# Two transformer layers on one core: every attention score product of the first four sequences is computed twice into the same banks

## The chip, the core and the metric

The kernel runs on one core of a Trainium2 chip. Five engines work side by side, each through its own list of instructions in a fixed order, and they wait for one another by semaphores: TensorE (PE in the profile; its weight loads are shown apart as PEld), VectorE (DVE), ScalarE (ACT), GpSimd (POOL) and SyncE (SP, which here issues transfers). TensorE writes its products to PSUM, eight banks of 512 fp32 values for each of 128 partitions, and DVE and ACT read them from there. The metric is the device time of one execution in microseconds (us), lower is better.

## What is computed

Two layers over x of 8 sequences, 512 positions, 128 features, all fp32 at the interface. Each layer is attention with 16 heads of 8 features and then a mixture of 8 experts; both are modulated by a small conditioning product. Layer 0 is what the change touches:

```python
h = _layernorm(x) * (1 + ca) + sa
qkv = jnp.einsum('bnd,ed->bne', h, w_qkv).reshape(b, n, 3, 16, 8)
q, k, v = (qkv[:, :, i].transpose(0, 2, 1, 3) for i in range(3))
attn = jax.nn.softmax(jnp.einsum('bhid,bhjd->bhij', q, k) * SCALE, axis=-1)
out = jnp.einsum('bhij,bhjd->bhid', attn, v)
x = x + ga * (out.transpose(0, 2, 1, 3).reshape(b, n, 128) @ w_out.T + b_out)
h = _layernorm(x) * (1 + cb) + sb
x = x + gb * ffn(h)      # gate, best 2 of 8 experts, one shared expert
```

Layer 1 has the same form, with a causal mask in the attention.

## The kernel before

**Steps.** Each sequence of each layer is a pass i, 0 to 7 for layer 0 and 8 to 15 for layer 1. A pass goes through normalisation (`p_...`), projection, scores, softmax, the product with the values, output projection (`t_...`), second normalisation and gate (`f_...`), the shared expert (`s_...`) and the routed experts (`x_...`). Passes overlap: while one is at its softmax, the next one's scores are computed, and the experts of earlier passes lie between them.

**Scores, computed two ways.** Queries and keys are split into three bf16 parts each, so that a product over 48 rows (`KA`) gives the score of one head to near fp32. For the softmax the kernel needs the maximum of each query's row first. So there is one score product with queries on the partitions, for the maximum alone (`score`, line 834), and a second one with keys on the partitions and three more rows that subtract the maximum (`bscore`, line 856), whose exponential goes into the product with the values.

- A unit `("score", i, f, pr, t)` is one half f of the heads, one of four pairs of heads pr and one of four tiles of 128 queries t: 32 units to a pass of layer 0. It opens two neighbouring PSUM banks and fills each with one matmul, 48 rows by 128 queries against 512 keys. The two matmuls of a unit (a = 0, 1) use different rows of the array. The last matmul raises the semaphore `score`.
- `rowmax` (line 1082, DVE) waits for that semaphore, reduces both banks (128 partitions by 1024 values) and by that frees them.
- After a half of the heads, `max_turn` (line 846) transposes the maxima; a chain over ACT, DVE, POOL and DMA brings them to the tiles QS.
- `bscore` (line 856) also opens two banks; `expo` (line 1429, ACT) takes the exponential of both into ES and frees them; `pv` (line 873) multiplies four heads of ES by the values, eight records in the trace to a unit.

Other rows that matter: line 748 is any dense projection (`product`), line 905 the gate's product, line 1075 the split of a projection on DVE, line 1354 the normalisation on ACT.

**What sets the order.** `plan()` lists every step with its engine, an estimated weight, an urgency (with tables of nudges) and its predecessors; `Plan.settle()` walks this list greedily and fixes each engine's order, and which banks each step opens. A step that opens banks waits for the steps that emptied them (`open_banks`). The weight of a `score` step in this plan is `0.01 + 0.22 * n / 512`.

The loop that issues a score unit:

```python
for t1, c, n in parts:
    for a in range(2):
        r = 64 * a
        mm = eng.matmul(psum[:, bank[u][a], c:c + n], QS[m][r:r + KA, pr, 128 * t1:128 * t1 + 128],
                        KS[m][r:r + KA, pr, 0:n], start=True, stop=i < NB)
...
mm.then_inc(s["score"], 1)
```

Of the kernel before, what the change touches and what calls it, by code (L numbers as in the profile page):

```python
# [13 lines left out]
NB, S, D = 8, 512, 128  # L14
# [27 lines left out]
KA, KB = 6 * DH, 6 * DH + 3  # L42
# [175 lines left out]


PIPE, WAKE = 1.0, 0.65  # L220
WARM = 12, 3, 3
LATER, SPARE = 0.6, 0.05
WEARLY = 0.2
# [313 lines left out]
def program(nc, xin, cT, wm, w0, we, ws, w1, wr1, wr2, wy, bo, out):  # L537
    ctx = ExitStack()
    with ctx:
# [22 lines left out]
        codeq = sb("codeq", [128, 128], BF16)  # L562
        codek = sb("codek", [128, 128], BF16)
# [3 lines left out]
        QS = [sb(f"QS{i}", [128, 4, S], BF16) for i in range(NSTK)]  # L567
        KS = [sb(f"KS{i}", [128, 4, S], BF16) for i in range(NSTK)]
# [60 lines left out]
        psum = ctx.enter_context(nc.psum_tensor("ps", [128, 8, 512], F32))  # L629
# [30 lines left out]
        todo, bank, emptied, _, strips = plan()  # L660
# [19 lines left out]
        for k in UNITS:  # L680
            m = (UNIT[k] if LAYER[k[0]] == 0 else k[1]) % (NST if LAYER[k[0]] == 0 else 2)
# [60 lines left out]
        def _(eng):  # L742
# [22 lines left out]
            for u in todo["PE"]:  # L765
# [4 lines left out]
                elif k in ("p_turn", "f_turn"):  # L770
                    w, i = (0, u[1]) if k == "p_turn" else (1, u[1])
# [3 lines left out]
                    for t in range(NT):  # L775
                        mm = eng.transpose(ps(*u)[:, 128 * t:128 * t + 128], xn[w][:, t, :], ident[:, :])  # L776
                    mm.then_inc(s[k], 1)
                elif k == "m_mm":
# [4 lines left out]
                    for c in range(6):  # L783
                        if l == 0:
                            warm(1)
                        mm = eng.matmul(ps(*u)[:, 8 * c:8 * c + 8], wms[l][c // 3][:, 128 * (c % 3):128 * (c % 3) + 128],
                                        cs[:, l, 0, :], start=True, stop=True)
                    mm.then_inc(s["m_mm"], 1)
                elif k == "m_gm":
# [4 lines left out]
                    for n, c in enumerate((2, 3, 4, 5)):  # L794
                        mm = eng.matmul(ps(*u)[0:8, 128 * n:128 * n + 128], cs[:, l, 0, :],
                                        wms[l][c // 3][:, 128 * (c % 3):128 * (c % 3) + 128], start=True, stop=True)
                    mm.then_inc(s["m_gm"], 1)
                elif k == "w_mm":
# [4 lines left out]
                               start=True, stop=True).then_inc(s[k], 1)  # L803
                elif k == "p_proj":
                    i, n = u[1:]
# [6 lines left out]
                elif k == "p_v":  # L812
                    i = u[1]
# [4 lines left out]
                    for t in range(NT):  # L818
                        mm = product(u, ps(*u)[:, 128 * t:128 * t + 128], hP[:, 128 * t:128 * t + 128],
                                        ws[:, W["v"]:W["v"] + 128], start=True, stop=True)  # L820
                    mm.then_inc(s[k], 1)
                elif k == "score":
                    i, f, pr, t = u[1:]
                    m = (2 * i + f) % NSTK

                    parts = [(t, 0, S)] if i < NB else [(t, 0, 128 * (t + 1))] if t > 1 else [(0, 0, 128), (1, 128, 256)]
                    q.wait_ge(*(on("early", i) if (i, f) == (0, 0) and pr < 2 else on("stack", i, f)))
                    open_banks(u)
                    if i >= NB:
                        q.wait_ge(s["ld", "c_code"], 32)  # L830
                    for t1, c, n in parts:
                        for a in range(2):
                            r = 64 * a
                            mm = eng.matmul(psum[:, bank[u][a], c:c + n], QS[m][r:r + KA, pr, 128 * t1:128 * t1 + 128],  # L834
                                            KS[m][r:r + KA, pr, 0:n], start=True, stop=i < NB)
                        if i >= NB:
                            for a in range(2):
                                r = 64 * a
                                mm = eng.matmul(psum[:, bank[u][a], c + n - 128:c + n], codeq[r:r + 64, :], codek[r:r + 64, :],  # L839
                                                start=False, stop=True)  # L840
                    mm.then_inc(s["score"], 1)
                elif k == "max_turn":
                    i, f = u[1:]
# [3 lines left out]
                elif k == "bscore":  # L847
                    i, f, g, j, pp = u[1:]
                    pr, m = 2 * g + pp, (2 * i + f) % NSTK
                    q.wait_ge(*on("max_ld", i, f))  # L850
                    q.wait_ge(s["ld", "c_ks"], 32 * NSTK)
                    open_banks(u)
                    for j1, c, q0 in key_tiles(i, j):
                        for a in range(2):
                            r = 64 * a
                            mm = eng.matmul(psum[:, bank[u][a], c:c + S - q0], KS[m][r:r + KB, pr, 128 * j1:128 * j1 + 128],  # L856
                                            QS[m][r:r + KB, pr, q0:S], start=True, stop=i < NB)
                        if i >= NB:
                            for a in range(2):
                                r = 64 * a  # L860
                                mm = eng.matmul(psum[:, bank[u][a], c:c + 128], codek[r:r + 64, :], codeq[r:r + 64, :],  # L861
                                                start=False, stop=True)
                    mm.then_inc(s["bscore"], 1)
                elif k == "pv":
                    i, g, j = u[1:]
# [4 lines left out]
                    for j1, c, q0 in key_tiles(i, j):  # L870
                        for a in range(4):
                            q.wait_ge(*on("expo", i, g // 2, g % 2, j, a // 2))
                            mm = eng.matmul(psum[32 * a:32 * a + 9, b, q0:S], VS[i % 3][:, j1, 4 * g + a, :],  # L873
                                            ES[(2 * EXP[i, g, j] + a // 2) % NES][:, a % 2, c:c + S - q0],
                                            start=(j1 == 0), stop=(j1 == NT - 1), skip_group_check=True)
                    mm.then_inc(s["pv"], 1)
                elif k == "v_turn":
# [3 lines left out]
                    for t in range(NT):  # L881
                        mm = eng.transpose(ps(*u)[:, 128 * t:128 * t + 128], US[g % 2][:, 128 * t:128 * t + 128], ident[:, :])
# [1047 lines left out]
```

## Time and profile before

| | us |
|---|---|
| median of 3 timed runs | 1061.68 (1061.51 to 1062.42) |
| the profiled execution, its own time | 1055.22 |
| its span in the trace | 1053.5 |
| PE busy | 976.7 (93%), 10743 matmuls |
| DVE busy | 824.4 (78%) |
| ACT busy | 743.0 (71%) |
| POOL busy | 454.5 (43%) |
| mean granted clock of TensorE | 0.967 |

The profile gives, for each engine, the busy time; TensorE's granted clock as a share of full speed (1.00 is 2.4 GHz, 0.50 is 1.2 GHz); and the chain of work that ended last, followed back from the end. How to read the views used below:

- The table by stretches has, for each stretch, its length, then the busy time and the count of instructions in brackets for PE, PEld, DVE, ACT and POOL, then the granted clock, the share of the DMA engines and GB/s.
- In the timeline a row gives start, length, engine, line, operation, tiles written and read, and in square brackets how long the engine was idle before it and who ended that. Neighbours of one line are merged: x2 is one score unit, x4 two, x8 one `pv` unit.
- In the chain a row gives start, length, engine, tile, line, count.

### The profile page before, as it was taken

The page shows a single profiled execution, that of the slowest core. Times are in us where ns is not written, and L with a number is a line of the kernel's source. Part 1 is how long each engine was busy: PE and PEld are TensorE (multiplying, and loading weights), DVE is VectorE, ACT ScalarE, POOL GpSimd, SP SyncE. Part 2 cuts the span into 40 slices and gives each one's busy share as a digit, 9 for nine tenths or more (in the row PEclk, how much of TensorE's full clock was granted, in tenths as well). Part 3 has the DMA queues.
Part 4 walks back from the last instruction along what each step waited for, and adds up shares of the span by engine and source line. Part 5 has one row for each costly group of instructions (what it writes and reads, how often), then busy time and mean ns, then how long its engine had stood idle before and what let it go on. Part 6 is the DMA issues. An engine that isn't in the chain of part 4 may idle for free.

```text
span 1053.5 us, 27436 instructions
## 1 busy us (share of the span) xinstructions
PE 976.7 (93%) x10743; PEld 529.7 (50%) x10743; DVE 824.4 (78%) x1672; ACT 743.0 (71%) x1225; POOL 454.5 (43%) x545
## 2 busy tenths in 40 slices
PE   7678898879999999999999999999999999999997
PEld 5211222222645455345655666666765555455565
DVE  6888899787999888678977688777877567677456
ACT  4347876668575766987577775666866988877864
POOL 5130121144024435641344742456644566836553
PEclk9858998899999999999999999999999989999999
DMA  6832525254664686584765896777887857411000
GB/s 186 209 115 53 144 73 147 77 168 128 186 204 121 216 247 178 157 246 147 244 203 165 259 278 196 223 208 227 262 260 227 234 167 183 111 62 56 33 12 21
DMA packets 120480, 174.73 MB, mean 166 GB/s; under 512 B 19896, under 2 KB 84280, under 8 KB 120352
## 3 DMA queue, kind: packets, MB, share of 16 engines
q1 hardware_dynamic: 114096, 159.87, 51.3%
q0 software_dynamic: 5680, 12.33, 4.0%
q8 instruction: 85, 1.39, 0.6%
q10 hardware_dynamic: 576, 0.79, 0.3%
q14 instruction: 43, 0.35, 0.1%
HBM read 114.21 MB, written 58.59 MB: 164 GB/s over the span
## 4 chain that ended last, share of the span: by engine, by line
PE 58%; DVE 20%; DMA 7%; ACT 6%; issue 5%; POOL 3%; SPq 1%; POOLq 0%; DVEq 0%; ACTq 0%
PE ps L748 19%; PE ps L873 13%; DVE nm L1082 12%; PE ps L750 8%; PE ps L856 7%; PE ps L834 6%; ACT ES L1429 3%; DMA gr<-d_y,pos 2%; DMA d_h<-hx,pos 1%; ACT xn L1354 1%; DMA d_h<-r,pos 1%; PE ps L776 1%; PE ps L905 1%; PE ps L839 1%; DMA DR<-d_r 1%
## 5 line engine op out<-in xcount | busy, mean ns | idle before, releaser
L1082 DVE TENSOR_REDUCE nm<-ps 128x2 f32<-128x1024 f32 (+3 forms) x512 | 504.6, 1019 | 106.9 <-PE ps L839 63.0
L1429 ACT ACTIVATE ES<-ps 128x1024 f32<-128x1024 f32 (+1 forms) x448 | 418.1, 961 | 104.4 <-PE ps L856 67.2
L873 PE MATMUL ps<-ES,VS 128*9 128x512 f32 (+3 forms) x2048 | 223.2, 522 | 0.4 <-DVE r L1268 0.2
L834 PE MATMUL ps<-KS,QS 48*128 48x512 bf16 (+3 forms) x1024 | 173.4, 354 | 31.0 <-DVE nm L1082 19.5
L856 PE MATMUL ps<-QS,KS 51*128 51x512 bf16 (+3 forms) x1024 | 168.6, 348 | 12.7 <-DVE nm L1082 6.4
L834 PEld LDWEIGHTS ps<-KS,QS 48*128 48x128 bf16 x1024 | 49.1, 94 | 145.9 <-DVE nm L1082 51.1
L856 PEld LDWEIGHTS ps<-QS,KS 51*128 51x128 bf16 x1024 | 50.2, 94 | 137.1 <-ACT ES L1429 44.7
L748 PE MATMUL ps<-hsT,wst 128*128 128x128 f32 x784 | 111.1, 285 | 2.8 <-DVE r L1275 1.6
L1657 POOL DMA_INDIRECT gr<-d_y,pos x80 | 83.3, 1041 | 64.2 <-DMA gr<-d_y,pos 35.7
L748 PEld LDWEIGHTS ps<-hsT,wst 128*128 128x128 f32 x784 | 95.2, 191 | 21.2 <-issue 17.4
L1583 POOL TENSOR_TENSOR sp<-sr,sp 128x512 bf16<-128x512 f32 x32 | 37.2, 1171 | 85.2 <-ACT sp L1390 85.1
L873 PEld LDWEIGHTS ps<-ES,VS 128*9 128x9 f32 x2048 | 37.9, 89 | 66.8 <-issue 57.1
L1468 ACT ACTIVATE tx<-ps 128x384 f32<-128x384 f32 x92 | 44.9, 488 | 34.4 <-PE ps L748 20.8
L1633 POOL DMA_INDIRECT d_h<-hx,pos x40 | 40.4, 1010 | 65.5 <-DMA d_h<-hx,pos 33.4
L1680 POOL TENSOR_TENSOR ya<-ya,yS 128x512 f32<-128x512 f32 x35 | 45.0, 1285 | 46.0 <-DVE yS L1317 45.9
L1633 POOL DMA_INDIRECT d_h<-r,pos x40 | 39.4, 985 | 44.7 <-DMA d_h<-r,pos 27.5
L1354 ACT ACTIVATE xn<-X,rs 128x128 f32<-128x128 f32 x128 | 52.5, 485 | 8.6 <-POOL rs L1579 7.2
L1587 POOL TENSOR_TENSOR nmp<-nmr,nmp 32x128 bf16<-32x128 f32 x32 | 14.0, 437 | 96.7 <-ACT nmp L1408 96.3
L839 PE MATMUL ps<-codek,codeq 64*128 64x128 bf16 x512 | 52.6, 218 | 0.0
L750 PE MATMUL ps<-hsT,wst 128*32 128x128 f32 x1464 | 49.2, 274 | 1.3 <-issue 1.2
L750 PEld LDWEIGHTS ps<-hsT,wst 128*32 128x32 f32 x1464 | 40.0, 110 | 19.7 <-issue 16.8
L861 PE MATMUL ps<-codeq,codek 64*128 64x128 bf16 x512 | 49.7, 218 | 0.1
(229 smaller groups left out, 1541.8 us busy)
## 6 DMA issues: line engine op xcount, KB each, us to landing
wst<-we SPq DMA_DIRECT2D x92, 576.0 KB
d_u<-US SPq DMA_DIRECT2D x60, 256.0 KB
KS<-d_k SPq DMA_DIRECT2D x62, 192.0 KB, 4.8
QS<-d_q SPq DMA_DIRECT2D x62, 192.0 KB, 5.4
hs<-d_h SPq DMA_DIRECT2D x25, 256.0 KB
d_y<-ys SPq DMA_DIRECT2D x25, 256.0 KB, 5.6
d_q<-sp SPq DMA_DIRECT2D x16, 384.0 KB, 3.0
d_k<-sp SPq DMA_DIRECT2D x16, 384.0 KB, 3.7
```

The source lines that it names most:

```text
L748: return eng.matmul(to, lhsT, rhs, start=start, stop=stop)
L750: mm = eng.matmul(to[r:r + 32, :], lhsT[:, r:r + 32], rhs, start=start, stop=stop, skip_group_check=True)
L834: mm = eng.matmul(psum[:, bank[u][a], c:c + n], QS[m][r:r + KA, pr, 128 * t1:128 * t1 + 128], KS[m][r:r + KA, pr, 0:n], start=True, stop=i ...
L839: mm = eng.matmul(psum[:, bank[u][a], c + n - 128:c + n], codeq[r:r + 64, :], codek[r:r + 64, :], start=False, stop=True)
L856: mm = eng.matmul(psum[:, bank[u][a], c:c + S - q0], KS[m][r:r + KB, pr, 128 * j1:128 * j1 + 128], QS[m][r:r + KB, pr, q0:S], start=True, ...
L861: mm = eng.matmul(psum[:, bank[u][a], c:c + 128], codek[r:r + 64, :], codeq[r:r + 64, :], start=False, stop=True)
L873: mm = eng.matmul(psum[32 * a:32 * a + 9, b, q0:S], VS[i % 3][:, j1, 4 * g + a, :], ES[(2 * EXP[i, g, j] + a // 2) % NES][:, a % 2, c:c + ...
L1082: ins = eng.tensor_reduce(nm[f][:, :].rearrange("p (a c) -> p a c", a=2)[:, :, 4 * pr + t1], ps2("score", i, f, pr, t)[:, :, c:c + n], AX. ...
L1354: ins = eng.activation(xn[w][:, t, :], X[:, NT * b + t, :], ACT.Identity, bias=rs[:, m, 2, t:t + 1], scale=rs[:, m, 1, t:t + 1])
L1429: eng.activation(ES[(2 * n + pp) % NES][:, :, 0:w], ps2("bscore", i, f, g, j, pp)[:, :, 0:w], ACT.Exp, scale=SC1 if i >= NB else SC0).then ...
L1633: eng.indirect_dma_start(out=d_h[:, :], out_offset=bass.IndirectOffsetOnAxis(ap=pos[p % 2][:, c, t8:t8 + 1], axis=0), in_=hx[t8 // NT][:, ...
L1657: eng.indirect_dma_start(out=gr[m][:, :], out_offset=None, in_=d_y[p][:, :], in_offset=bass.IndirectOffsetOnAxis(ap=pos[p % 2][:, c, t8:t8 ...
```

## The change

For the passes i = 0 to 3 the loop that issues a score unit runs twice. A table `MORE_S` holds a 1 for each of the 128 units of these passes (i, f, pr, t); a second table, `MORE_B`, of the same kind for `bscore`, is empty. Both matmuls of a unit are issued a second time, with the same operands into the same two banks and with start=True, so that the second result overwrites the first with the same values. The semaphore is raised by the last matmul of the second round. The planner's weights, its order and the banks are as before.

```diff
 PIPE, WAKE = 1.0, 0.65
+MORE_S = {
+    (0, 0, 0, 0): 1, (0, 0, 0, 1): 1, (0, 0, 0, 2): 1, (0, 0, 0, 3): 1, (0, 0, 1, 0): 1, (0, 0, 1, 1): 1,
...
+    (3, 1, 3, 2): 1, (3, 1, 3, 3): 1,
+}
+MORE_B = {
+
+}
...
                     open_banks(u)
                     if i >= NB:
                         q.wait_ge(s["ld", "c_code"], 32)
-                    for t1, c, n in parts:
-                        for a in range(2):
-                            r = 64 * a
-                            mm = eng.matmul(psum[:, bank[u][a], c:c + n], QS[m][r:r + KA, pr, 128 * t1:128 * t1 + 128],
-                                            KS[m][r:r + KA, pr, 0:n], start=True, stop=i < NB)
...
+                    for _ in range(1 + MORE_S.get(u[1:], 0)):
+                        for t1, c, n in parts:
                             for a in range(2):
                                 r = 64 * a
...
+                                mm = eng.matmul(psum[:, bank[u][a], c:c + n], QS[m][r:r + KA, pr, 128 * t1:128 * t1 + 128],
+                                                KS[m][r:r + KA, pr, 0:n], start=True, stop=i < NB)
...
                     mm.then_inc(s["score"], 1)
```

Nothing else in the program moves. On TensorE, where the softmax of pass 0 meets the scores of pass 1, there stood in a row (L834 `score`, L856 `bscore`, L873 `pv`; in the program's own order a `pv` unit has four matmuls):

```order
L856 MATMUL ps<-QS,KS 128x512 x2
L834 MATMUL ps<-KS,QS 128x512 x2
L873 MATMUL ps<-ES,VS 9x512 x4
L856 MATMUL ps<-QS,KS 128x512 x2
L834 MATMUL ps<-KS,QS 128x512 x2
L856 MATMUL ps<-QS,KS 128x512 x2
L834 MATMUL ps<-KS,QS 128x512 x2
L873 MATMUL ps<-ES,VS 9x512 x4
```

And now, at the same place (the lines of the file have moved by 29 to 31):

```order
L887 MATMUL ps<-QS,KS 128x512 x2
L864 MATMUL ps<-KS,QS 128x512 x4
L904 MATMUL ps<-ES,VS 9x512 x4
L887 MATMUL ps<-QS,KS 128x512 x2
L864 MATMUL ps<-KS,QS 128x512 x4
L887 MATMUL ps<-QS,KS 128x512 x2
L864 MATMUL ps<-KS,QS 128x512 x4
L904 MATMUL ps<-ES,VS 9x512 x4
```

Each x2 of `score` has become x4, and nothing has changed its place: 256 matmuls and 256 weight loads more in all. The orders of the other engines are the same instructions in the same sequence.

## Rows read from the trace of the kernel before

**Rows 1.** The page: busy time of PE, and the granted clock in 40 slices.

```profile
PE 976.7 (93%) x10743; PEld 529.7 (50%) x10743; DVE 824.4 (78%) x1672; ACT 743.0 (71%) x1225; POOL 454.5 (43%) x545
...
PEclk9858998899999999999999999999999989999999
```

**Rows 2.** Table by stretches, cut where the granted clock changes.

```profile
28.76:45.83 17.07, 11.76 (x60) 5.20 (x58) 15.55 (x18) 7.75 (x16) 2.58 (x10) 1.00 0.70 200
45.83:76.55 30.72, 20.40 (x76) 3.46 (x76) 28.08 (x29) 12.03 (x18) 9.53 (x12) 0.50 0.54 149
76.55:93.62 17.07, 14.14 (x106) 2.89 (x102) 14.15 (x12) 13.14 (x16) 0.00 (x0) 1.00 0.34 80
93.62:100.44 6.82, 6.38 (x29) 0.96 (x31) 5.87 (x7) 4.01 (x6) 0.42 (x1) 0.50 0.01 3
100.44:172.12 71.68, 62.70 (x462) 18.66 (x454) 64.41 (x91) 55.10 (x74) 12.07 (x15) 1.00 0.42 113
172.12:178.95 6.83, 6.00 (x17) 1.45 (x15) 6.10 (x8) 4.50 (x7) 0.42 (x1) 0.50 0.34 104
199.43:206.26 6.83, 6.83 (x22) 3.35 (x21) 3.21 (x13) 2.89 (x6) 0.97 (x2) 0.50 0.13 46
```

**Rows 3.** Timeline: score units back to back, at the two clocks.

```profile
29.99 0.61 PE L834 MATMUL ps<-KS,QS 48*128 48x512 bf16 x4
...
99.00 1.04 PE L834 MATMUL ps<-KS,QS 48*128 48x512 bf16 x4
```

**Rows 4.** Timeline, 45.9 to 49.5 us: DVE and PE while pass 0 has only scores.

```profile
44.86 5.74 DVE L1082 TENSOR_REDUCE nm<-ps 128x2 f32<-128x1024 f32 x5
...
47.26 0.61 PE L834 MATMUL ps<-KS,QS 48*128 48x512 bf16 x2 [0.53 <-DVE nm L1082]
```

**Rows 5.** Timeline, 82.5 to 88.6 us: one turn of score, softmax and value product.

```profile
82.93 0.39 PE L834 MATMUL ps<-KS,QS 48*128 48x512 bf16 x2 [0.68 <-ACT ES L1429]
...
83.25 1.04 PE L873 MATMUL ps<-ES,VS 128*9 128x512 f32 x8
...
84.23 0.39 PE L856 MATMUL ps<-QS,KS 51*128 51x512 bf16 x2
...
84.46 0.38 PE L834 MATMUL ps<-KS,QS 48*128 48x512 bf16 x2
...
84.67 1.94 ACT L1429 ACTIVATE ES<-ps 128x1024 f32<-128x1024 f32 x2 [0.87 <-PE ps L856]
...
84.88 2.52 DVE L1082 TENSOR_REDUCE nm<-ps 128x2 f32<-128x1024 f32 x2 [0.29 <-PE ps L834]
85.74 0.39 PE L834 MATMUL ps<-KS,QS 48*128 48x512 bf16 x2 [0.68 <-ACT ES L1429]
```

**Rows 6.** The chain that ended last: its first and last score unit of passes 0 to 3.

```profile
30.06 0.34 PE ps L834 x2
...
228.44 0.39 PE ps L834 x2
```

**Rows 7.** The chain that ended last: pieces at either clock.

```profile
97.24 1.82 PE ps L873 x8
...
101.54 0.98 PE ps L873 x8
...
174.46 1.71 PE ps L748 x2
...
199.55 1.83 PE ps L873 x8
201.38 1.81 PE ps L905 x8
203.18 1.92 PE ps L748 x2
```

**Rows 8.** Timeline of DVE, 180 to 188 us: reductions without a gap.

```profile
181.43 5.77 DVE L1082 TENSOR_REDUCE nm<-ps 128x2 f32<-128x1024 f32 x5
```

**Rows 9.** Table by stretches: scores alone, and score and bscore in turn.

```profile
41.50:45.80 4.30, 1.30 (x8) 0.29 (x6) 4.30 (x4) 0.00 (x0) 0.00 (x0) 1.00 0.63 164
90.30:93.60 3.30, 2.35 (x16) 0.63 (x14) 3.10 (x3) 3.30 (x5) 0.00 (x0) 1.00 0.83 173
```

More of the change, by code:

```diff
@@ L830, in _ @@
                         q.wait_ge(s["ld", "c_code"], 32)
-                    for t1, c, n in parts:
-                        for a in range(2):
-                            r = 64 * a
-                            mm = eng.matmul(psum[:, bank[u][a], c:c + n], QS[m][r:r + KA, pr, 128 * t1:128 * t1 + 128],
-                                            KS[m][r:r + KA, pr, 0:n], start=True, stop=i < NB)
-                        if i >= NB:
+                    for _ in range(1 + MORE_S.get(u[1:], 0)):
+                        for t1, c, n in parts:
                             for a in range(2):
                                 r = 64 * a
-                                mm = eng.matmul(psum[:, bank[u][a], c + n - 128:c + n], codeq[r:r + 64, :], codek[r:r + 64, :],
-                                                start=False, stop=True)
+                                mm = eng.matmul(psum[:, bank[u][a], c:c + n], QS[m][r:r + KA, pr, 128 * t1:128 * t1 + 128],
+                                                KS[m][r:r + KA, pr, 0:n], start=True, stop=i < NB)
+                            if i >= NB:
+                                for a in range(2):
+                                    r = 64 * a
+                                    mm = eng.matmul(psum[:, bank[u][a], c + n - 128:c + n], codeq[r:r + 64, :], codek[r:r + 64, :],
+                                                    start=False, stop=True)
                     mm.then_inc(s["score"], 1)
@@ L852, in _ @@
                     open_banks(u)
[L853 to L858, printed above, removed]
+                    for _ in range(1 + MORE_B.get(u[1:], 0)):
+                        for j1, c, q0 in key_tiles(i, j):
                             for a in range(2):
                                 r = 64 * a
-                                mm = eng.matmul(psum[:, bank[u][a], c:c + 128], codek[r:r + 64, :], codeq[r:r + 64, :],
-                                                start=False, stop=True)
+                                mm = eng.matmul(psum[:, bank[u][a], c:c + S - q0], KS[m][r:r + KB, pr, 128 * j1:128 * j1 + 128],
+                                                QS[m][r:r + KB, pr, q0:S], start=True, stop=i < NB)
+                            if i >= NB:
+                                for a in range(2):
+                                    r = 64 * a
+                                    mm = eng.matmul(psum[:, bank[u][a], c:c + 128], codek[r:r + 64, :], codeq[r:r + 64, :],
+                                                    start=False, stop=True)
                     mm.then_inc(s["bscore"], 1)
```

20 rows, old and new, of the table MORE_S are left out of this document.

## The prediction, as it was written before the changed kernel had run

> **What bounds the kernel now.** I read the page first: PE is busy 93% of the span, the other engines less, and its granted clock is not full everywhere; the third of the 40 slices shows 0.5 [rows 1]. So the next view is the table cut where the clock changes. Between 28.8 and 229 us, where all scores of passes 0 to 3 lie, the clock is at 0.50 (1.2 GHz) in four stretches: 30.7 us from 45.8, and 6.8 us each from 93.6, 172.1 and 199.4, together 51 us; elsewhere it is at 1.00 (2.4 GHz) [rows 2]. That matters, because the change adds only TensorE work, and more work before a fall of the clock can prevent it.
>
> Then the timeline. While pass 0 has nothing but scores, DVE reduces without a gap, 1.13 us for each unit (5.74 us less some overlap, for five), and PE sits idle half a microsecond before each unit, released by DVE [rows 4]: DVE is the bound there. Where the softmax of one pass meets the scores of the next, the turn repeats every 2.81 us (82.93 to 85.74): ACT ends an exponential, this frees the banks of a score unit, behind it on PE stands the value product (line 873), behind that a bscore pair, and this feeds ACT again [rows 5]. The loop goes through PE and ACT, and one of its two score units is in it. DVE has slack in it: two reductions take 2.52 of 2.81 us.
>
> **What a copy costs.** Two units back to back take 0.61 us, one takes 0.39 (at 1.00); so a unit that follows another without a pause costs 0.61 - 0.39 = 0.22 us. At 0.50 it is 1.04 - 0.61 = 0.43 us [rows 3, 4, 5]. The copy is just that, a second unit behind the first, so 128 copies are 128 x 0.22 = 28 us of PE time at the full clock. Most of it must lie in idle time, or the change is plainly bad.
>
> Hidden copies. (a) Scores alone at the full clock: a unit is ready half a microsecond before DVE wants it; 0.22 fits. (b) The same at 0.50: PE starts when a reduction ends and has about 1.04 us until DVE wants the result, while unit and copy take 0.61 + 0.43 = 1.04 plus about 0.1 for the two hand-overs. It misses by 0.11 us. Four units (46.1 to 49.6 us) have no second one in reserve: 4 x 0.11 = **0.4 us**. (c) In the turn of [rows 5] the unit at 84.46 delays only the second bscore pair, whose exponential waits for ACT anyway: hidden by 0.5 us.
>
> Exposed copies. I followed the chain that ended last from 28 to 229 us and counted its pieces of line 834. From the first to the last [rows 6] there are 36 units of passes 0 to 3. Four of these (69.1, 95.3, 176.7 and 179.3 us) wait for DVE or precede a wait for it, so 32 remain, 23 of them between 74 and 129 us, where the turn above is the bound: 32 x 0.22 = **7.0 us**. A second amount is not on today's chain: where PE has no pause for several units, copies add up until DVE must wait. DVE's five reductions from 181.4 us on run without a gap [rows 8], while PE brings one unit in each 1.5 us and is itself without a pause; eight copies there are 1.7 us, of which the reserve of ready units takes up all but about 0.5. In the same way I take 0.8 for 132 to 159 us and 0.4 for 165 to 170 us: **1.7 us**. Bounds: nothing, if the reserves hold, and 5.5 us, if the 25 or so copies of these places all show. I take the low third since DVE's own pauses there are short but many.
>
> **What the clock gives back.** First the rows. At 45.8 us the clock falls after PE had done one unit each 1.13 us (1.30 us busy in 4.30). At 93.6 it falls after one score and one bscore pair each 1.13 us (2.35 busy in 3.30) [rows 9]. With copies, the first place looks as the second does now, two pairs in each 1.13 us; so I expect **the fall at 45.8 to stay**. The second gets three pairs; the long full-clock stretch to 172 us with 62.7 us busy of 71.7 [rows 2] shows the clock held by work that is not much denser than that. So I expect the falls at 93.6, 172.1 and 199.4 to go; the last units ahead of each of them (90.6 to 92.9, 169.5 to 171.8, 196.3 and 198.9 us) all get a copy.
>
> The Trainium skill ("TensorE: Matmul & The Clock Gate", section "Why this matters for your kernels") puts drops of the clock down to long idle gaps between bursts of matmuls. The trace disagrees here: at 45.8 us no pause of PE was longer than a microsecond or so, and the clock fell all the same.
>
> And the rise comes earlier. In the low stretch from 45.8, PE at 0.50 does unit and copy in 1.04 of each 1.13 us, all but without a pause, and that is what it did before it rose at 76.5 and 100.4. I take the rise for 53 to 60 us instead of 76.5.
>
> What this is worth, stretch by stretch. A value product takes 1.82 us at 0.50 and 0.98 at 1.00 [rows 7].
> - 45.8 to 76.5: until 71 us DVE is the bound, nothing gained. Behind it two value products (2 x 0.84), and five pairs and a transpose that take twice as long (some 1.2 us): **2.8 us**.
> - 93.6 to 100.4: DVE bounds until 96.3; behind that one value product and part of a second (1.05), three units and a transpose (0.9): **1.95 us**. Its three copies are in the 32 above.
> - 172.1 to 178.9: two dense products at 1.71 [rows 7], half of it each at the full clock, make 1.7 us on PE, but DVE has work of its own for all but **1.3 us**.
> - 199.4 to 206.3: value product, gate and shared expert follow on PE without a pause, 1.83 + 1.81 + 1.92 = 5.56 us [rows 7]; at the full clock 0.98 for the first, half for the others with a tenth or two of latency, 3.06: **2.5 us**.
> Together 8.55 us. With the fall at 199.4 gone, the thin stretch at 216 to 220 us, in which DVE works out the positions of tokens, may bring a fall of its own; DVE is the bound until 228, so I charge **0.5 us**.
>
> **The sum.** 0.4 + 7.0 + 1.7 + 0.5 - 8.55 = +1.05 us. Against the profiled execution's 1055.22 this gives 1056.3. The timed runs are 6.5 us longer than that execution; I carry the difference over: 1061.7 + 1.1 = **1062.8 us**. From 229 us on everything is as before and follows at the same distance.
>
> **Rivals.**
> 1. *The clock doesn't answer as I think, slower.* The falls at 172.1 and 199.4 stay. Then 3.8 us of gain is lost, and copies near them cost 0.43 instead of 0.22 (three or four, 0.7 us), with the 0.5 for the later fall not due: +1.05 + 3.8 + 0.7 - 0.5 = +5.0, 1066.7 us. It decides as soon as one of the two stays. For it: the last place holds only two units in the time ahead of the fall, and at 196.9 to 198.3 PE waits for ACT, which no copy fills. Against: a third of PE's idle time ahead of the other one is filled. The exposed copies running to their upper bound lead to the same side (+3.8).
> 2. *The low clock costs more in the timed runs than in the profiled one, faster.* They are 6.5 us longer, about three low stretches at 1.3 to 2.8 us. If two of these lie below 229 us and the copies remove them as well, 4 to 5 us are gained: 1.05 - 4.5, 1058.2 us. For it: PE is nearly idle at several places (168, 209, 214 to 219 us), where a fall hangs on how they happen to lie. Against: no row shows such a run.
> 3. *No effect on the clock at all.* This is what the skill's rule about long gaps would give, since the copies fill no long gap. Then the four stretches stay as they are and only costs remain: 0.4 + 7.0 + 1.7 and some 2.5 for copies at 0.43: +11.6, 1073.3 us.
> 4. *The copies don't cost what I think*, because a matmul repeated into the same bank could wait for the first. No row has this; the nearest, units into different banks, gives 0.22. A wait of half of it more would add 32 x 0.11 = 3.5 us, to 1066.3 us. It goes with the first rival.
>
> **How the numbers follow.** A measurement of this kernel can tell some 0.2% (2.1 us) from no change. Chances: forecast 0.45 (its own spread 1060 to 1066, for the 1.7 could be 0 to 5.5), rivals 1 and 4 0.25, rival 2 0.25, rival 3 0.05. Within the forecast's case 0.34 falls within 0.2%, 0.04 below and 0.07 above. So faster 0.29, same 0.34, slower 0.37. The range takes in rivals 1 and 2: 1057.5 to 1068.
>
> **What would show it.** Line 834's records in passes 0 to 3: 512 instead of 256. The granted clock: still a fall near 46 us, a rise before 62, then none below 0.9 until 215 us. The turn of [rows 5]: 3.03 us instead of 2.81. The value product that starts at 77.4 us: 1.4 to 2.1 us earlier, after which the lead melts until 129 us, where work lies about 1.7 us later than before. The stretch behind the f_gate of pass 0 (199.4 us): made up by 2.5 us. Wrong it would be if the clock still falls at 93.6 or 172, if no fall comes at 46 (then 0.4 us less), or if DVE's reductions show waits for line 834 all over 130 to 190 us.

## The result, and the profile of the changed kernel

The changed kernel takes 1067.94 us (median of 14 runs, 1063.44 to 1072.27), the kernel before 1063.64 us beside it (14 runs, 1061.51 to 1068.22). The ratio is 1.0044 with an interval of 1.0023 to 1.0065: **slower by 0.44%, some 4.7 us** (4.3 between the medians). The forecast was 1062.8 us, no difference that can be told, so it missed by more than the change is worth. The time itself lies just inside the range; that is luck, as the range reached so far for mechanisms that did not come.

The profiled execution took 1069.11 us (span 1067.4). The one of before took 1055.22, well under all of its timed runs, so these two traces are 13.9 us apart where the timed runs are 4.7 apart. Comparing the two spans would mislead. I compared the start of the same DVE instruction in both traces instead, stretch by stretch, and trust that only up to 240 us, where the last copied unit is done.

The page, to be read against [rows 1]: 256 matmuls more, 22.6 us more of busy PE, and among the first ten slices two at 0.8 where there were four.

```profile
PE 999.3 (94%) x10999; PEld 536.3 (50%) x10999; DVE 826.4 (77%) x1672; ACT 743.3 (70%) x1225; POOL 454.9 (43%) x545
...
PEclk9859999989999999999999999999999999999999
```

The table by stretches of the changed kernel, cut where the clock changes (from : to, length; busy time and instructions of PE, PEld, DVE, ACT, POOL; granted clock; share and GB/s of DMA). It answers to [rows 2]:

```profile
29.20:46.30 17.10, 13.91 (x84) 5.70 (x84) 15.20 (x18) 7.34 (x16) 2.58 (x10) 1.00 0.64 196
46.30:77.00 30.70, 26.34 (x110) 4.53 (x110) 28.06 (x28) 10.35 (x16) 9.13 (x11) 0.50 0.57 149
77.00:223.80 146.80, 133.33 (x1059) 38.97 (x1057) 127.25 (x190) 106.00 (x140) 23.16 (x30) 1.00 0.33 91
223.80:230.60 6.80, 6.27 (x28) 1.09 (x28) 5.17 (x7) 1.57 (x2) 5.43 (x7) 0.50 0.67 208
```

The falls at 93.6, 172.1 and 199.4 are gone, as forecast. The long one at 46 us is there, and lasts 30.7 us as before instead of ending by 62. A new one of 6.8 us has come at 223.8, where the kernel before had none.

The lag behind the kernel before, summed up from its start (us; an ordinary table made from the two traces; "start" is what the two executions already differ by ahead of the first copy):

```
before's time          30.4   42.6   71.2   77.5   90.5  128.5  171.7  181.4  203.2  214.3  240.8
changed, first trace  +0.40  +0.83  +1.79  +1.77  +3.07  +4.46  +6.54  +5.35  +4.85  +4.07  +6.35
```

What the copies cost shows in the turn of [rows 5]. Timeline of the changed kernel at the same place (start, length, engine, line and operation, records; in brackets the idle time before it and what ended it):

```profile
85.14 0.60 PE L864 MATMUL ps<-KS,QS 48*128 48x512 bf16 x4 [0.47 <-ACT ES L1460]
...
85.67 1.05 PE L904 MATMUL ps<-ES,VS 128*9 128x512 f32 x8
...
86.88 0.60 PE L864 MATMUL ps<-KS,QS 48*128 48x512 bf16 x4
...
88.16 0.60 PE L864 MATMUL ps<-KS,QS 48*128 48x512 bf16 x4 [0.47 <-ACT ES L1460]
```

A unit is four records and 0.60 us instead of two and 0.39, and the turn takes 88.16 - 85.14 = 3.02 us instead of 2.81. Only one of its two copies is in the loop: 0.21 us.

### The profile page after: what moved, and what is told of

It reads as the page before. It is cut to its first block, busy times and chain, and to the rows that moved or that the text cites. A ratio compares the mean times of both kernels' runs of the same rounds, so it can differ in the third digit from the quotient of the medians.

```text
span 1067.4 us, 27948 instructions
## 1 busy us (share of the span) xinstructions
PE 999.3 (94%) x10999; PEld 536.3 (50%) x10999; DVE 826.4 (77%) x1672; ACT 743.3 (70%) x1225; POOL 454.9 (43%) x545
## 3 DMA queue, kind: packets, MB, share of 16 engines
q8 instruction: 87, 1.43, 0.6%
## 4 chain that ended last, share of the span: by engine, by line
PE 60%; DVE 15%; DMA 10%; ACT 7%; issue 5%; POOL 3%; SPq 0%; POOLq 0%; DVEq 0%; ACTq 0%
PE ps L777 19%; PE ps L904 13%; PE ps L864 8%; DVE nm L1113 8%; PE ps L779 7%; PE ps L887 7%; DMA gr<-d_y,pos 5%; ACT ES L1460 3%; ACT xn L1385 2%; DMA d_h<-hx,pos 1%; DMA d_y<-ys 1%; DMA d_h<-r,pos 1%; PE ps L805 1%; PE ps L969 1%; PE ps L936 1%
## 5 line engine op out<-in xcount | busy, mean ns | idle before, releaser
L864 PE MATMUL ps<-KS,QS 48*128 48x512 bf16 (+3 forms) x1280 | 204.7, 368 | 20.4 <-DVE nm L1113 10.2
L864 PEld LDWEIGHTS ps<-KS,QS 48*128 48x128 bf16 x1280 | 56.0, 96 | 149.0 <-DVE nm L1113 46.6
L1614 POOL TENSOR_TENSOR sp<-sr,sp 128x512 bf16<-128x512 f32 x32 | 37.2, 1173 | 88.7 <-ACT sp L1421 88.6
L1618 POOL TENSOR_TENSOR nmp<-nmr,nmp 32x128 bf16<-32x128 f32 x32 | 14.0, 437 | 100.6 <-ACT nmp L1439 100.4
L1469 ACT ACTIVATE US<-ps 128x512 f32<-128x512 f32 x64 | 38.1, 596 | 16.3 <-PE ps L904 15.9
```

## The experiments

All of them change the table `MORE_S` alone (how many copies a unit gets), or nothing. Units are numbered in the order in which PE takes them, 1 to 128 in passes 0 to 3, and 129 to 256 in passes 4 to 7. The runs fall on three occasions, on which the kernel before itself took 1080.88 us (the first four), 1075.79 (the next four) and 1073.65 (the last two). Where a kernel was executed only once, its time therefore says little, and it is read by its trace. Lags are those of the same DVE instruction behind the first trace of before, and this table stands for all of them:

```
before's time        30.4   71.2   77.5   90.5  128.5  171.7  181.4  203.2  214.3  240.8
e1_first33          +0.43  +1.83  +1.23  +1.23  +2.29  +2.29  +2.75  +1.20  +0.43  +2.79
e2_other95          +1.49  +1.49  +2.40  +3.69  +5.09  +7.17  +5.99  +5.49  +4.72  +9.23
e3_three_first      +0.80  +3.32  +1.26  +1.30  +1.01  +1.01  +0.97  -0.71  -1.48  -0.08
e4_ahead12          +1.50  +4.05  +3.33  +3.55  +1.99  +1.98  +0.80  -0.74  -1.51  +2.77
e5_placed           +0.23  +2.92  +0.31  +0.57  +0.28  +0.28  -0.91  -2.45  -3.22  -1.84
e6_passes4to7       +0.35  +0.35  +0.39  +0.39  +0.41  +0.40  +0.42  +0.42  +0.43  +0.86
e7_changed_again    +1.01  +2.40  +2.35  +3.65  +5.04  +7.12  +5.94  +5.44  +4.66  +6.93
e8_before_again     +1.55  +4.11  +3.39  +3.39  +3.03  +3.03  +2.80  +1.13  +0.36  +1.17
e9_ahead22          +1.56  +4.18  +3.51  +3.72  +2.16  +2.17  +0.98  -0.55  -1.32  -0.35
e10_changed_timed   +0.54  +2.03  +1.78  +3.07  +4.47  +6.55  +5.37  +4.87  +4.10  +4.66
```

### The first 33 copies alone

```diff
 MORE_S = {
...
-    (0, 1, 3, 2): 1, (0, 1, 3, 3): 1, (1, 0, 0, 0): 1, (1, 0, 0, 1): 1, (1, 0, 0, 2): 1, (1, 0, 0, 3): 1,
...
-    (3, 1, 3, 2): 1, (3, 1, 3, 3): 1,
+    (0, 1, 3, 2): 1, (0, 1, 3, 3): 1, (1, 0, 0, 0): 1,
 }
```

> Copies only for the first 33 score units (up to 69 us, where DVE bounds), none for the other 95. Theory A (costs show on PE's chain, the clock answers to what PE did just before): up to 77 us this kernel runs like the changed one, with the clock at 0.50 from about 46 to 77 us and DVE's work about 2.4 us later than in the kernel before; then the falls near 94, 172 and 200 us come back, because their units have no copy, and the lag stays at 2 to 3 us at 230 us. Rival B (the copies of the first 33 units are what keeps the clock up later, by some longer memory of the clock): no fall between 77 and 220 us, and the lag at 230 us turns into a lead of 4 us or so.

The trace follows the changed kernel up to 71 us: +1.40 us net of the start, and again no rise before 76.7. From there on it follows before: falls at 97.2 and 175.7 are back, each 3.6 us later than in before's first trace. So the first copies do not act on the later falls, and it is the copies behind them that remove these.

```profile
97.20:104.00 6.80, 6.46 (x29) 0.82 (x33) 5.09 (x6) 1.69 (x5) 0.42 (x1) 0.50 0.03 7
175.70:182.50 6.80, 6.28 (x17) 1.60 (x17) 5.39 (x8) 4.39 (x7) 0.42 (x1) 0.50 0.36 106
216.70:230.30 13.60, 11.54 (x50) 1.58 (x48) 11.28 (x19) 5.63 (x6) 7.18 (x9) 0.50 0.62 224
```

What neither of the two theories had: with no copy anywhere near it, the fall at 199 stayed away too (the lag sinks from 2.75 at 181 to 0.43 at 214), and one twice as long came at 216.7 in its place and took 2.36 back. One fall can swap for the other without a copy.

### The other 95 copies alone

```diff
 MORE_S = {
-    (0, 0, 0, 0): 1, (0, 0, 0, 1): 1, (0, 0, 0, 2): 1, (0, 0, 0, 3): 1, (0, 0, 1, 0): 1, (0, 0, 1, 1): 1,
...
-    (0, 1, 3, 2): 1, (0, 1, 3, 3): 1, (1, 0, 0, 0): 1, (1, 0, 0, 1): 1, (1, 0, 0, 2): 1, (1, 0, 0, 3): 1,
+    (1, 0, 0, 1): 1, (1, 0, 0, 2): 1, (1, 0, 0, 3): 1,
...
 }
```

> Copies only for units 34 to 128 (from 74 us on). Theory A: the same low stretch from 46 to 77 us as before, nothing later than before by 77 us; after it no fall until about 220 us; DVE's work at 230 us is later than before by 6.35 (the changed kernel) less 2.4 (its first 33 copies), so by 4 us. Rival B: falls at 94, 172, 200 us as before, and then a lag of 8 us or more.

Between 77 and 214 us it is the changed kernel once more: from +2.40 to +4.72, that is +2.32, where the changed kernel has +2.30 (1.77 to 4.07). No fall from 79 to 225.8. At 240 us it stands 7.7 us behind, net of its start, where some 4 had been expected. The surplus is the late fall, 10.2 us long here. By 77.5 us it is already 0.91 us late net of its start, where nothing was expected: its first copies, from 74 us on, still lie in the low stretch.

```profile
79.00:225.80 146.80, 132.74 (x1053) 38.98 (x1049) 127.34 (x192) 104.77 (x138) 23.83 (x30) 1.00 0.34 93
225.80:236.00 10.20, 9.57 (x42) 1.71 (x44) 6.63 (x7) 2.54 (x3) 6.02 (x7) 0.50 0.71 258
```

### Two copies in place of one, for units 11 to 33

```diff
 MORE_S = {
-    (0, 0, 0, 0): 1, (0, 0, 0, 1): 1, (0, 0, 0, 2): 1, (0, 0, 0, 3): 1, (0, 0, 1, 0): 1, (0, 0, 1, 1): 1,
...
-    (3, 1, 3, 2): 1, (3, 1, 3, 3): 1,
+    (0, 0, 2, 2): 2, (0, 0, 2, 3): 2, (0, 0, 3, 0): 2, (0, 0, 3, 1): 2, (0, 0, 3, 2): 2, (0, 0, 3, 3): 2,
...
+    (0, 1, 2, 3): 2, (0, 1, 3, 0): 2, (0, 1, 3, 1): 2, (0, 1, 3, 2): 2, (0, 1, 3, 3): 2,
 }
```

> Two copies (each product three times) for units 11 to 33, from 42.7 us on, while DVE bounds; no copy elsewhere. Theory A: at the full clock unit and copies take 0.39 + 0.44 us of the about 1.0 us that PE has, so they cost nothing; three pairs in each 1.13 us keep the clock at 1.00 through 46 us, or bring it back before 60 us; DVE's work at 77 us is 1.5 to 2.8 us EARLIER than before, the falls at 94, 172 and 200 us stay. Rival C (the low stretch isn't what holds up 71 to 77 us, or three pairs are still too little): the clock falls at 46 us as before; then three pairs take 0.61 + 0.86 = 1.47 us at 0.50, PE bounds, and DVE's work at 77 us is later by 20 x 0.3 = 6 us or, with an early rise, 2 us.

The step of the prediction on trial is that a denser PE ends the low stretch early. With three products per unit PE works 0.82 of each 1.13 us at the full clock, and the fall at 46 does not come at all. Two shorter ones come, at 53.6 and 67.2. Ahead of the first PE waited for DVE around the turn of the maxima (line 858), ahead of the second for two other results of DVE:

```profile
50.41 0.82 PE L846 MATMUL ps<-KS,QS 48*128 48x512 bf16 x6 [0.40 <-DVE nm L1095]
51.45 0.28 PE L858 MATMUL ps<-ident,nm 128*32 128x128 f32 x1 [0.22 <-DVE nm L1095]
52.59 5.24 PE L846 MATMUL ps<-KS,QS 48*128 48x512 bf16 x30 [0.85 <-DVE nm L1095]
...
65.44 0.39 PE L869 MATMUL ps<-QS,KS 51*128 51x512 bf16 x2 [0.46 <-DVE sr L1088]
66.48 0.82 PE L846 MATMUL ps<-KS,QS 48*128 48x512 bf16 x6 [0.65 <-DVE nm L1095]
```

```profile
53.60:57.00 3.40, 3.40 (x18) 1.24 (x16) 2.57 (x3) 0.97 (x3) 2.64 (x3) 0.50 0.55 176
57.00:67.20 10.20, 6.86 (x54) 1.89 (x50) 9.98 (x10) 3.25 (x5) 6.02 (x8) 1.00 0.58 179
67.20:74.10 6.90, 6.90 (x34) 1.94 (x30) 5.88 (x6) 2.34 (x3) 0.50 (x1) 0.51 0.21 69
```

In these low stretches PE is busy without any pause (3.40 of 3.40 and 6.90 of 6.90 us), and they end after 3.4 and 6.9 us. In the changed kernel's stretch it is busy 26.34 of 30.70 and the clock rises only at its end. The clock does answer to more work on PE, then, but one copy for each unit is not enough. And it does not pay: at 77 us the lag is +0.46 net of the start where a gain of 1.5 to 2.8 was expected, since three products at 0.50 take longer than DVE's 1.13 us and push the lag up to 3.3 on the way. Of the later falls, all expected to stay, two came (98.0 and 173.0 us); the one near 199 did not, though no copy is near it, and one of 6.8 us came at 217.4 as in e1.

### Twelve copies ahead of the falls alone

```diff
 MORE_S = {
-    (0, 0, 0, 0): 1, (0, 0, 0, 1): 1, (0, 0, 0, 2): 1, (0, 0, 0, 3): 1, (0, 0, 1, 0): 1, (0, 0, 1, 1): 1,
...
-    (3, 1, 3, 2): 1, (3, 1, 3, 3): 1,
+    (1, 0, 2, 3): 1, (1, 0, 3, 0): 1, (1, 0, 3, 1): 1, (1, 0, 3, 2): 1, (1, 0, 3, 3): 1, (3, 0, 0, 1): 1,
+    (2, 1, 3, 2): 1, (3, 0, 0, 2): 1, (2, 1, 3, 3): 1, (3, 0, 0, 3): 1, (3, 1, 0, 2): 1, (3, 1, 0, 3): 1,
 }
```

> Copies only for 12 units that lie just ahead of the three later falls: 44 to 48, 96 to 100, 115 and 116. Theory A: the low stretch from 46 to 77 us as before, no lag at 90 us; the falls at 94, 172 and 200 us do not come; the copies cost 3 x 0.22 us; so DVE's work at 210 us is 1.95 + 1.3 + 2.5 - 0.7 = 5 us earlier than before. A fall may come at 216 to 224 us and take back 2 us. Rival D (the clock is set by work over a longer time than these few copies): one or more of the three falls stays, each worth 1.3 to 2.5 us.

These are units 44 to 48, 96 to 100, 115 and 116, the last ones ahead of 93.6, 172.1 and 199.4 us, where DVE or ACT bounds. No fall from 79 to 215.6, and the lag goes from +3.55 at 90.5 to -1.51 at 214.3: **5.06 us gained** on the first trace of before, for an expected 5. How much of this before can gain by itself is seen further down, in its second trace. Then 215.6 to 232.6 is low, and 4.3 of it is lost again by 240 us:

```profile
79.00:215.60 136.60, 117.67 (x902) 34.15 (x899) 123.73 (x182) 103.60 (x138) 22.86 (x29) 1.00 0.36 96
215.60:232.60 17.00, 13.72 (x60) 1.97 (x58) 12.57 (x18) 8.16 (x9) 9.33 (x10) 0.50 0.54 193
```

Ahead of it PE paused 0.6 us for ACT. The longer pauses, 1.4 us and nearly one, come inside it; they are for DVE, which is working out the positions of tokens.

```profile
214.66 0.39 PE L867 MATMUL ps<-QS,KS 51*128 51x512 bf16 x2 [0.62 <-ACT ES L1440]
...
218.27 0.61 PE L844 MATMUL ps<-KS,QS 48*128 48x512 bf16 x2 [1.38 <-DVE nm L1093]
...
220.26 0.61 PE L844 MATMUL ps<-KS,QS 48*128 48x512 bf16 x2 [0.96 <-DVE nm L1093]
220.80 1.89 PE L884 MATMUL ps<-ES,VS 128*9 128x512 f32 x8
```

### Copies placed everywhere that seemed worth it

```diff
 MORE_S = {
-    (0, 0, 0, 0): 1, (0, 0, 0, 1): 1, (0, 0, 0, 2): 1, (0, 0, 0, 3): 1, (0, 0, 1, 0): 1, (0, 0, 1, 1): 1,
...
-    (3, 1, 3, 2): 1, (3, 1, 3, 3): 1,
...
+    (0, 1, 0, 0): 3, (0, 1, 0, 1): 3, (0, 1, 0, 2): 2, (1, 0, 0, 0): 2, (0, 1, 0, 3): 2, (0, 1, 1, 0): 2,
...
+    (3, 0, 0, 2): 1, (2, 1, 3, 3): 1, (3, 0, 0, 3): 1, (3, 1, 0, 2): 1, (3, 1, 0, 3): 1, (3, 1, 1, 0): 1,
+    (3, 1, 1, 1): 2, (3, 1, 1, 2): 2, (3, 1, 1, 3): 2, (3, 1, 2, 0): 4, (3, 1, 2, 1): 2, (3, 1, 2, 2): 2,
+    (3, 1, 2, 3): 2, (3, 1, 3, 0): 2, (3, 1, 3, 1): 2, (3, 1, 3, 2): 2,
 }
```

> Copies placed by what e3 and e4 showed, in spots where DVE bounds: two copies for most of units 11 to 33 and three beside the pauses of TensorE there (17, 18, 28, 29), one for 44 to 48, 96 to 100 and 115 to 117, one or two for 118 to 127 and four for 121. Theory A (copies are free where DVE bounds and buy back the clock): no stretch at 0.50 longer than 4 us between 45 and 230 us; DVE's work at 77 us 1 to 2.8 us earlier than before, at 210 us 5 to 8 us, at 240 us 4 to 7 us earlier; in time 0.3 to 0.6% faster than before. Rival E (an earlier finish of passes 0 to 3 does not reach the end, since later stretches wait for transfers): the lead at 240 us is there, and the time is within 0.2% of before.

This keeps the twelve, gives units 11 to 33 mostly two copies (three for 17, 18, 28 and 29), and adds copies to units 117 to 127 against the late fall. The late fall is gone: no low stretch between 206 and 260 us, and at 240 the kernel leads by 1.84 us, 2.1 net of its start. But two short falls at 52.8 and 66.5 remain (in the first PE is again busy without a pause, 3.40 us of 3.40), and one of 3.4 us at 97.2, which the five copies of units 44 to 48 did not prevent here. The lead at 240 us is well short of the 4 to 7 us that were expected, and at 77.5 us there is none. Timed, it is 1072.57 us to 1075.79, ratio 0.9985 (0.9952 to 1.0018): no difference that can be told, where 0.3 to 0.6% faster was expected.

```profile
52.80:56.20 3.40, 3.40 (x20) 1.19 (x16) 3.19 (x4) 1.40 (x3) 2.64 (x3) 0.50 0.67 199
56.20:66.50 10.30, 7.17 (x56) 2.08 (x54) 9.58 (x10) 3.15 (x5) 5.62 (x8) 1.00 0.52 166
```

### The same copies in passes 4 to 7, where the clock does not fall

```diff
 MORE_S = {
-    (0, 0, 0, 0): 1, (0, 0, 0, 1): 1, (0, 0, 0, 2): 1, (0, 0, 0, 3): 1, (0, 0, 1, 0): 1, (0, 0, 1, 1): 1,
...
-    (3, 1, 3, 2): 1, (3, 1, 3, 3): 1,
+    (4, 0, 0, 0): 1, (4, 0, 0, 1): 1, (4, 0, 0, 2): 1, (4, 0, 0, 3): 1, (4, 0, 1, 0): 1, (4, 0, 1, 1): 1,
...
+    (7, 1, 3, 2): 1, (7, 1, 3, 3): 1,
 }
```

> No copies in passes 0 to 3, one for each of the 128 units of passes 4 to 7 (232 to about 490 us), where the kernel before has its clock at 1.00 throughout. It measures what 128 copies cost where the clock has nothing to give back. Theory A: TensorE is denser there than in passes 0 to 3, so more than the 9 us that passes 0 to 3 paid: 128 x 0.22 = 28 us is the most, 15 to 25 us expected as added lag between 232 and 500 us. Rival F (copies are mostly hidden by DVE's reductions everywhere): under 10 us.

Up to 233 us it is the kernel before, with its falls at 94.0, 172.6 and 199.9, and a lag of +0.64. By 500 us the lag is 21.6, almost 21 us more, the largest step of the study. PE had no room there:

```profile
232.00:500.00 268.00, 258.66 (x2692) 129.28 (x2691) 206.52 (x366) 188.80 (x294) 101.33 (x119) 1.00 0.60 177
```

Its chain of waits (start, length, what the end of the program hung on) shows the copy in it, a score unit of 0.54 us beside a bscore of 0.22, one behind the other and nothing but PE:

```profile
305.71 0.11 PE ps L876
305.82 0.54 PE ps L864 x4
306.36 0.22 PE ps L887 x2
306.57 0.79 PE ps L779 x24
307.37 0.86 PE ps L904 x8
308.22 0.54 PE ps L864 x4
```

128 copies at 0.22 are 28 us at most. How much of the 21 is theirs is not settled to a microsecond: of the other three traces of this occasion, none with a copy there, e5 fell back by 1.9 us from 240 to 500 us, e7 by 3.5 and e8 by 11.4. That leaves 9 to 19 us for the copies, so the 15 to 25 us that were expected are not confirmed, and the rival's "under 10" is only just not met. Even 9 is about twice what the change costs in passes 0 to 3, and here no clock gives anything back.

### The changed kernel and the kernel before once more

Both unchanged, to see what one more execution of each does.

> The changed kernel once more. Theory A: low stretch from 46 to 77 us, none from 77 to about 220, one at about 224 us; DVE's work 6 us late at 240 us against the first trace of before. The second part of the lag in the first trace (7.6 us between 812 and 900 us) is a matter of single slow transfers and will be of another size and at another place.

The changed kernel repeats its first trace: low from 46.8 to 77.5 and from 224.3 to 231.1, the same lags but for the start, +6.93 at 240 us (5.9 net of the start, as in the first).

```profile
224.30:231.10 6.80, 6.22 (x28) 1.14 (x28) 5.17 (x7) 1.49 (x2) 5.45 (x7) 0.50 0.66 214
```

> The kernel before once more. If the falls of the clock lie the same in every execution, they come at 46, 94, 172 and 199 us again and DVE's work at 240 us is within 0.5 us of the first trace. If they hang on how the execution happens to lie, there are others (near 216 to 220 us above all), and the time at 240 us differs by 2 us or more.

The kernel before does not repeat. Its falls lie at 34.7, 48.4, 99.6, 174.7, 222.5 and 263.4, and the one at 199 is missing:

```profile
34.70:41.60 6.90, 6.48 (x18) 3.03 (x17) 5.51 (x9) 0.44 (x1) 0.00 (x0) 0.51 0.52 176
222.50:225.90 3.40, 3.24 (x16) 0.36 (x14) 2.81 (x3) 0.54 (x1) 2.54 (x4) 0.50 0.77 204
```

So the trace on which the prediction rests had one of at least two patterns, and the fall at 199 (2.5 us of the expected gain) is not in every execution of before. From 90.5 to 214.3 us this trace gains 3.03 us on the first one without a single copy (3.39 to 0.36). Of the 5.06 us of e4 only 2.03 are left against it, and they are lost again by 240 us, where e4 falls back by 4.28 us and this trace by 0.81. The fall at 34.7 also explains why e4 and e9, which have it too, stand 4.1 us behind at 71 us: it is no effect of their copies.

### Twenty-two copies: ahead of the falls, and against the late one

These are the twelve copies of e4, one for each of the units 117 to 120 and 122 to 124, and three for unit 121.

```diff
 MORE_S = {
-    (0, 0, 0, 0): 1, (0, 0, 0, 1): 1, (0, 0, 0, 2): 1, (0, 0, 0, 3): 1, (0, 0, 1, 0): 1, (0, 0, 1, 1): 1,
...
-    (3, 1, 3, 2): 1, (3, 1, 3, 3): 1,
...
+    (2, 1, 3, 2): 1, (3, 0, 0, 2): 1, (2, 1, 3, 3): 1, (3, 0, 0, 3): 1, (3, 1, 0, 2): 1, (3, 1, 0, 3): 1,
+    (3, 1, 1, 0): 1, (3, 1, 1, 1): 1, (3, 1, 1, 2): 1, (3, 1, 1, 3): 1, (3, 1, 2, 0): 3, (3, 1, 2, 1): 1,
+    (3, 1, 2, 2): 1, (3, 1, 2, 3): 1,
 }
```

> As e4, copies only ahead of the falls and where DVE bounds, with the place near 216 to 224 us added: one copy for units 44 to 48, 96 to 100, 115 to 120 and 122 to 124, three for unit 121; none for the first 33 units. Theory A: the low stretch from 46 to 77 us as before, no fall at 94, 172, 200 or 216 to 224 us; between 90 and 214 us DVE's work gains 5 us on before, and at most 1.5 us are lost to 240 us; in time 0.2 to 0.5% faster than before. Rival E (later transfers and other falls of the clock swallow it): within 0.2%.

1071.63 us (12 runs) beside 1073.65 of before (23 runs): ratio **0.9971 (0.9944 to 0.9999), faster** by some 3 us, with an interval that only just leaves one out. It is the one kernel of the study that beats both, and with three kernels timed an interval so close to one may still be chance. The trace has 5.04 us gained from 90.5 to 214.3, as in e4, and from there to 240 us a loss of only 0.97. From 90.5 to 240.8 us it gains 4.07 us on the first trace of before and 1.85 on the second, which fits the timed 3. There is no low stretch from 79.3 to 860 us:

```profile
79.30:213.00 133.70, 116.16 (x891) 33.84 (x889) 120.89 (x179) 100.72 (x135) 20.34 (x27) 1.00 0.36 98
213.00:233.00 20.00, 14.18 (x106) 3.17 (x104) 16.28 (x24) 14.57 (x18) 10.90 (x11) 1.00 0.58 190
```

### The changed kernel, timed beside the last one

> The changed kernel on another occasion, beside the kernel before and e9. Theory A: its copies cost 9 us on TensorE's chain up to 240 us and get 6 back, so it is 5 to 6 us late at 240 us and 0.3 to 0.6% slower than before. Rival G (the first measurement caught a difference in the late transfers, not in the copies): within 0.2%.

No edit. The changed kernel takes 1077.16 us (12 runs), at a ratio to before 1.0038 (1.0013 to 1.0063), so the first result holds on another occasion. Up to 214 us its trace is the first one to 0.15 us, net of the start (+3.56 here, +3.67 there), but here **no fall comes at 224**: the lag is 4.66 at 240 us instead of 6.35, and less than the 5 to 6 expected, though the code is the same.

```profile
76.70:831.00 754.30, 711.37 (x8075) 376.79 (x8073) 608.14 (x1154) 523.65 (x835) 288.14 (x334) 1.00 0.61 182
```

## Why the prediction was wrong, and where it was right

That it could end slower was among the cases, and these made up the upper end of the range, but by other mechanisms (falls that stay, a wait for the same bank) than the one that came. The lag of the first trace at 240 us, 6.35 us, can now be taken apart and set beside the sum of +1.05:

```
term                                     predicted   measured   from
before the first copy                        -          +0.4    start of the trace
copies, to 214 us                          +9.1         +8.7    (3.07 - 0.40) + (4.07 - 3.07) + 5.06
copies, behind 214 us                      (in it)      +0.6    e10: 4.10 to 4.66, no fall there
falls at 94, 172 and 199 gone              -5.75        -5.06   e4 against the first trace
the stretch from 46 us ends early          -2.8          0      low to 77.0, e1 76.7, e7 77.5, e10 76.7
the swapped late fall                      +0.5         +1.7    (6.35 - 4.07) less the 0.6
sum                                        +1.05        +6.35
```

The second and the fourth line are only known together: e4's 5.06 is net of what its own twelve copies cost (0.7 us by its expectation), and the 8.7 is what the 116 others add to that.

**The price of a copy: right.** 0.22 us on a chain of PE work, nothing where DVE bounds. The turn grew by 0.21 us. Further on, where value products follow each other, the distance from one to the next is 187.16 - 185.43 = 1.73 us, and it was 183.05 - 181.53 = 1.52. The lag from 77.5 to 128.5 us grew by 2.7, and from there to 171.7 by 2.1. The count of units on the chain [rows 6] and the 1.7 us for reserves used up came to 9.1 together, and measured were 9.3, or some 10 with the twelve of e4. The fourth rival, a wait for the same bank, has nothing to stand on: a unit with its copy takes 0.60 us, as two units into different banks did [rows 3].

```profile
185.43 1.05 PE L904 MATMUL ps<-ES,VS 128*9 128x512 f32 x8
...
187.16 1.04 PE L904 MATMUL ps<-ES,VS 128*9 128x512 f32 x8
```

**That the falls at 94, 172 and 199 go: right** in all three traces of the changed kernel, but not all of it is the copies' doing. Near 94 to 100 us and near 172 to 176 us every trace without copies there has its fall (before twice, e1, e3, e6), and of the seven with copies there only e5 has one, at 97.2. The fall at 199 stands only in the first trace of before and in e6; e1, e3 and e8 lack it with no copy near. So its 2.5 us rest on one pattern of before, and the 5.06 for 5.75 is what the copies gain on that pattern; on the other it is 2.0. The first rival (two of them stay) and the third (the clock does not answer at all) fell with it. The Trainium skill ("TensorE: Matmul & The Clock Gate", section "Why this matters for your kernels") puts drops of the clock down to long idle gaps between bursts of matmuls. The traces disagree: in the kernel before, the longest pause of PE shortly ahead of the falls at 94, 172 and 199 was 0.52, 0.63 and 1.43 us, and copies that only shortened such pauses kept the clock up at the first two places, but for e5's one fall.

```profile
91.55 0.39 PE L856 MATMUL ps<-QS,KS 51*128 51x512 bf16 x2 [0.52 <-ACT ES L1429]
```

**That the stretch at 46 us ends early: the step that failed.** The prediction said that unit and copy fill "1.04 of each 1.13 us, all but without a pause", and that this is what PE did before it rose at 76.5 and 100.4. The words "all but" hid a difference: ahead of those two rises PE had worked with no pause at all for 5.3 and 5.2 us (71.2 to 76.5, 95.3 to 100.4). Timeline of the changed kernel from 46.9 us:

```profile
46.96 2.17 PE L864 MATMUL ps<-KS,QS 48*128 48x512 bf16 x8 [0.47 <-DVE nm L1113]
...
49.32 1.04 PE L864 MATMUL ps<-KS,QS 48*128 48x512 bf16 x4 [0.20 <-DVE nm L1113]
...
50.54 1.04 PE L864 MATMUL ps<-KS,QS 48*128 48x512 bf16 x4 [0.18 <-DVE nm L1113]
```

PE still pauses 0.2 us in each 1.22, since it waits for DVE to free the banks and DVE waits for PE: the two alternate, as the prediction's own 0.4 us for these units implied. The same stretch ends at 76.7 in e1 and e10 and at 77.5 in e7, so the missing rise is shown in four traces. With the third product of e3 and e5 the low stretches that start at 53.6 and 52.8 us end after 3.4 us.

That the pauses are the whole reason is not shown. After the turn of the maxima the changed kernel has five units ready, and PE works from 52.9 to 56.5 us without a pause at 0.50; the clock does not rise:

```profile
53.00:56.50 3.50, 3.49 (x16) 0.68 (x14) 3.48 (x5) 1.41 (x3) 2.32 (x3) 0.50 0.62 176
```

And in the low stretches from 199.4 (before) and 67.2 us (e3) PE never pauses, and they last 6.8 us, not 3.4.

The missing rise took 2.8 us out of the sum: half of the 5.3 us by which the first trace missed it, and most of the 3.0 to 3.7 us by which the timed runs did. The prediction's own sign shows it: the work near 77.4 us was to come 1.4 to 2.1 us earlier and came 1.8 later, and at 129 us it lay 4.5 us later instead of 1.7. The 2.8 us themselves were of the right size: in e5, where the clock is back at 69.9, the lag falls by 2.60 us from 71.2 to 77.5, but e5's extra copies had cost 2.69 by then.

**The late fall: right that it might come, wrong in its size.** It was charged at 0.5 us because DVE bounds until 228. In the first trace it reaches to 230.6, over a value product that stands on the chain:

```profile
222.22 0.39 PE L887 MATMUL ps<-QS,KS 51*128 51x512 bf16 x2 [0.20 <-ACT ES L1460]
223.77 1.03 PE L864 MATMUL ps<-KS,QS 48*128 48x512 bf16 x4 [1.15 <-DVE nm L1113]
...
226.72 1.89 PE L904 MATMUL ps<-ES,VS 128*9 128x512 f32 x8
```

It cost 1.7 us here and in e7 with a length of 6.8 us, 2.4 in e1 (13.6 us), 3.9 in e2 (10.2 us) and 4.3 in e4 (17.0 us), and nothing in e10. Such a fall must be priced by what follows within its whole length, not by what bounds at its start.

**The second rival** (more low stretches in before's timed runs, which the copies would remove too) found no support. Before's second trace does have one low stretch more below 229 us, at 34.7, but the changed kernel can have the same stretch (e4 and e9 show that copies behind it do not touch it), and the timed runs came out on the other side.

**From the trace to the timed runs.** Without start and late fall the changed kernel is 6.35 - 0.4 - 1.7 = 4.25 us behind; with the late fall it is 5.95. The timed differences are 4.7 (1067.94 - 1063.64 gives 4.3) and 1073.65 x 0.0038 = 4.1 us. That fits without anything behind 240 us. Net of the starts, e10 and e7 stand 4.5 and 6.3 us behind the second trace of before at 240 us, so the cost does not hang on which of its two traces is taken. The first two traces drift apart by another 7.4 us between 800 and 1048 us (from +6.53 to +13.90). That is no part of the change: before's own second trace falls back by 8.1 us over the same end (+21.13 to +29.21), so it is the first trace of before that was quick there. The chain of waits of the changed kernel holds a gather there that took 7.68 us; that such transfers are the cause is read from the chain, and was not tried apart.

```profile
818.69 7.68 DMA gr<-d_y,pos
```

**What stays open.** Which of its patterns the clock takes near 199, 216 and 224 us in a given execution is not settled: e1 swapped the falls with no copy near, before has a fall at 199 in one trace and none there in the other, and e10 and e7 differ at 224 with the same code. Nor is it known why every kernel without copies in passes 4 to 7, before included, fell back by another 8 to 20 us between 240 and 800 us on the later occasions; e6's size is uncertain by 10 us for that reason.

## What to carry to other kernels

Redundant products on TensorE pay only where another engine bounds and only just ahead of a fall of the clock: twelve such copies gained 5 us on one trace of the kernel before and 2 on the other, and the 116 others lost 9. Price a copy by its whole time wherever the chain runs through PE, and where there is no fall to prevent, leave it out. Before counting on an early rise of the clock, compare PE's pauses with those ahead of a rise in the same trace: here a pause of 0.2 us in each 1.22 went with no rise for 30.7 us. Take more than one trace of the kernel before to see which of its falls come each time. And compare two traces instruction by instruction up to where the edit ends, not by their spans.

## What the runs showed of the hardware that was not expected

- A matmul pair repeated into its own banks costs the same as one into others: 0.21 to 0.22 us at the full clock, 0.43 at half, with no wait for the first.
- The same code can have its low stretches in different places from one execution to the next (before: 93.6, 172.1, 199.4 in one, 99.6, 174.7, 222.5 in another), and their lengths come as 3.4, 6.8, 10.2, 13.6, 17.0 and 30.7 us.
- Ahead of the falls between 40 and 240 us the longest pause of PE was 0.4 to 1.4 us. The rises at 76.5 and 100.4 us of before came behind 5.3 and 5.2 us of work without a pause, and the one at 57.0 us of e3 ended a low stretch of 3.4 us without one; 3.6 us without a pause in the changed kernel, at half clock from 52.9 us, brought none.
